# Attention passes: five edge columns of a round copied out of a turned node table in SBUF instead of four of them being gathered by GpSimd and one by ScalarE's DMAs

## Chip, cores, metric

One Trainium2 chip, one core. The metric is the device time of one launch in microseconds (us), as the median over runs. Engine names: PE is TensorE, DVE VectorE, ACT ScalarE, POOL GpSimd, SP SyncE.

## What is computed

Four graph networks follow one another on 12,500 nodes of 64 features and 200,000 edges sorted by destination. The change touches the three attention layers in the middle (stages c3, c4 and c5 and what lies between them). Cut to its core, such a layer is:

```python
h = x @ W                                   # per node, 4 heads of 16
e = (h * a_s)[src] + (h * a_d)[dst]         # per edge and head (c3 adds a term of edge_attr)
e = leaky_relu(e, 0.2)
w = exp(e - segment_max(e, dst))
out = segment_sum(w * h[src], dst) / segment_sum(w, dst)
```

Every edge needs the row of its source node: 64 projected features and 4 scores. Nodes are laid out as node = p * 98 + c (128 partitions p, NC = 98 columns c), edges as edge = p * 1563 + t, so that one *column* t is 128 edges, one on each partition, with 128 unrelated source nodes.

## The kernel before, in words

**Tables.** The node stages (conv_to_gat, gat_to_gat) end in gat_back (L1396): for a block of up to eight node columns, PE turns pairs of columns of h (L1415), ACT copies the turned pair to a small buffer hn (L1435), PE multiplies it by wg = [W, W a_s, W a_d] for both nodes of the pair (L1426), and ACT copies the result to gt (L1441). gt is stored to g_tab in DRAM, one row of TG = 72 floats for a node (64 features, 4 source scores, 4 target scores); POOL also scatters the target scores to ad_start (L1457).

**An attention pass** is gat_edges (L1805). It takes the 1563 edge columns in NGRP = 98 groups of GW = 16 columns, through a ring of NY = 6 slots of the buffer y (slot = group mod 6). Six groups are a *round*; there are 16 rounds and two groups more, which are handled as four half pieces (LASTS). For each group:

- POOL fills the slot by one indirect DMA for each column (L1862), after the piece that used the slot six groups before has been weighted (`weighted`). It takes all columns but those of the list `taken`: SP fetches column 15 of slots 2 and 5, ACT column 14 of slot 5. So POOL has 93 of 96 columns of a round.
- SP fetches a column by loading 32 source places at a time into registers (L303) and issuing 128 one-row DMAs (L307). ACT does the same for its column in four parts of 32, in the first four groups of a round, each after its other work of the group (`group`, L2009).
- DVE's `step` (L1880 to L1943) adds the scores (L1894; in c3 also the edge term that PE made, L1899), applies the leaky relu (L1903), makes running maxima by four scans (L1909), carries the last one (L1918, which waits until ACT has sent the piece before), forms the exponents' arguments (L1921 to L1925), waits for ACT's exponentials (L1930), weights the rows (L1931), sums them by a scan over 1156 elements (L1938) and carries on (L1941).
- ACT's `weights` makes the exponentials (L1979, L1984), `send` waits for the scan and copies maxima and sums to `row` (L1992, L1993), and issues the store (L1996). In c3 it also issues the load of edge_attr (L1999).

The order is written out by hand on each engine, and each runs a hardware loop over rounds: DVE and ACT both go through the six groups of a round in one loop body. DVE and ACT are tied within a group: exponentials wait for `shifted` (L1925), weighting waits for the exponentials, sending waits for the scan. Nothing else is planned by cost.

**Between c2 and c3** stands block_diagonal (L1787), in which POOL cuts a small matrix with two instructions (L1798, L1801) while no other engine has work.

Of the kernel before, what the change touches and what calls it, by code (L numbers as in the profile page):

```python
# [18 lines left out]
F32 = mybir.dt.float32  # L19
I32 = mybir.dt.int32  # L20
# [5 lines left out]
P = 128  # L26
# [31 lines left out]
ACT_SLOT, ACT_K, NACT = NY - 1, GW - 2, NGRP // NY  # L58
NTABLE = NSYNC + NACT
# [9 lines left out]
    ln_squared ln_var ln_rooted ln_inverted ln_done w_made ones_set h_turned0 h_turned1 mixed0 mixed1 q_ready0  # L69
    q_ready1 edges_ready q_turned0 q_turned1 weighted0 weighted1 row_ready0 row_ready1 q_filled q_carried multiplied  # L70
    scored maxed m_carried shifted exps r_ready summed carried differed fix_steps agg_made0 agg_made1 agg_turned0
    agg_turned1 agg_copied0 agg_copied1 done0 done1 den inv inv_has skipped0 skipped1 gat_steps cut ad_filled
# [3 lines left out]
    norm_steps w_zeroed new_turned hn_ready g_mixed gt_ready skipped own_scored same_copied  # L76
""".split()
# [44 lines left out]
def by_pool(g, taken):  # L122

    return width(g) - taken.count(g % NY)
# [27 lines left out]
def over_wide_blocks(eng, body):  # L152

    with eng.Fori(0, NWBLK // 2) as i:
        for b in range(2):
            body(i, b)
    for b in range(NWBLK % 2):
        body(NWBLK // 2, b)

# [15 lines left out]
class Stage:  # L175
# [38 lines left out]
    def row_slots(self, fills, taken=(), cut=0):  # L214

        return [[self.dma(f"gathered_{slot}{part}", fill_of(slot, taken) * n - cut * part * (slot == HALVED[1]))
                 for part in range(1 + (slot in HALVED))] for slot, n in enumerate(fills)]

    def pass_slots(self, taken, ahead=0):

        return self.row_slots([len(range(slot, NGRP, NY)) - (slot < ahead) for slot in range(NY)], taken, CUT)
# [14 lines left out]
def build(nc, a, out):  # L236
# [149 lines left out]
    def begin(y, wq_t, bq, wk_t, bk, we_t):  # L386
# [35 lines left out]
        src_loaded, places_stored = st.dma("src_loaded", 32), st.dma("places_stored", 32)  # L422
# [17 lines left out]
        with nc.Block(no_gpsimd_drain=True) as block:  # L440
            @block.sync
            def _(sp):
# [7 lines left out]
                with nc.allow_non_contiguous_dma("single columns of src"):  # L450
                    by_column = a["src"].rearrange("(p t) -> t p", p=P)
                    sp.dma_start(src_i[0:NSYNC, :], by_column[(EVERY - 1) * GW + SYNC_K:EVERY * GW * NSYNC:EVERY * GW, :])\
                        .then_inc(src_loaded.h, 16)
                    sp.dma_start(src_i[NSYNC:NTABLE, :], by_column[ACT_SLOT * GW + ACT_K:NY * GW * NACT:NY * GW, :])\
# [74 lines left out]
            def _(v):  # L529
# [144 lines left out]
                v.wait_ge(*src_loaded(32))  # L674
# [675 lines left out]
    def gat_weights(st, w, a_src, a_dst, heads, edge=None):  # L1350


        wg, wr = st.sb("wg", [P, 2, TG]), st.sb("wr", [P, D])
# [1413 lines left out]
```

## Time and profile before

| | us |
|---|---|
| median of 3 runs (lowest, highest) | 13215.1 (13211.56, 13216.55) |
| the profiled execution, from its first to its last instruction | 13211.9 |
| POOL busy | 9802.5 (74%) |
| DVE busy | 6811.8 (52%) |
| ACT busy | 4061.7 (31%) |
| PE busy | 517.1 (4%) |
| POOL's gathers of the three passes (L1862), busy and issue gaps | 4291.3 + 1386.9 |

The profiled execution's span is 3.2 us below the median of the runs, which is a launch's time with what lies around the span. The page's busy shares are means over stages: the passes of the change take about 5,700 us of the span. In them POOL is busy for three quarters of the time, and the rest of its time is the gap between one gather and the next. Busy time counts neither register instructions nor loads of registers nor the issue of a DMA; the queue of an engine is written with a q behind its name (ACTq, SPq).

### The profile page before, as it was taken

What the parts mean: (1) busy time and instruction counts of PE and PEld (TensorE: products, weight loads), DVE (VectorE), ACT (ScalarE), POOL (GpSimd) and SP (SyncE); (2) the same over time, 40 slices, a digit from 0 to 9 for tenths busy, and PEclk for the clock granted to TensorE, in tenths of its full rate; (3) what the DMA queues carried; (4) which work ended last, traced back from release to release, by engine and by line L of the source; (5) the groups of instructions that cost most, each with busy time, mean ns of one, the idle gap of its engine ahead of it and who ended that gap; (6) DMA issues with size and microseconds to landing.
All of it is one profiled execution on the core that took longest, in us unless ns stands there. A gap on an engine that the chain in (4) does not pass through costs nothing. (4 is left out here: it accounts for less than half of the span.)

```text
span 13211.9 us, 103483 instructions
## 1 busy us (share of the span) xinstructions
PE 517.1 (4%) x1768; PEld 338.5 (3%) x1768; DVE 6811.8 (52%) x10645; ACT 4061.7 (31%) x4014; POOL 9802.5 (74%) x10362
## 2 busy tenths in 40 slices
PE   3000001100000200000010000000000000000001
PEld 1000000100000200000000000000000000000000
DVE  2777876377777533333333333343333336656656
ACT  4333333233333311111111111111111113666663
POOL 7777776777777677777777777777777776777775
PEclk9999999555555655555555555555555555555555
DMA  8445444344444222222212222222222223444443
GB/s 334 120 123 129 123 123 107 90 123 123 123 122 124 64 66 65 63 65 66 63 45 61 61 63 62 60 49 58 62 61 61 61 63 89 160 160 156 162 160 116
DMA packets 977609, 1316.81 MB, mean 100 GB/s; under 512 B 660939, under 2 KB 676770, under 8 KB 963551
## 3 DMA queue, kind: packets, MB, share of 16 engines
q10 hardware_dynamic: 558595, 803.76, 18.8%
q0 software_dynamic: 334400, 373.85, 14.8%
q1 hardware_dynamic: 83996, 134.02, 2.8%
q14 instruction: 604, 4.95, 0.1%
q8 instruction: 14, 0.23, 0.0%
HBM read 651.23 MB, written 659.53 MB: 99 GB/s over the span
## 5 line engine op out<-in xcount | busy, mean ns | idle before, releaser
L1862 POOL DMA_INDIRECT c_y<-g_tab,srcs x4545 | 4291.3, 944 | 1386.9 <-issue 1386.9
L2318 POOL DMA_INDIRECT c_y<-h_tab,srcs x1547 | 1461.0, 944 | 506.4 <-issue 471.4
L824 POOL DMA_INDIRECT c_y<-h_tab,srcs x1531 | 1444.9, 944 | 467.1 <-issue 467.1
L824 POOL DMA_INDIRECT first_y<-h_tab,srcs x1452 | 1370.6, 944 | 445.2 <-issue 442.6
L1894 DVE TENSOR_TENSOR c_s<-c_y,c_ad 128x64 f32<-128x64 f32 x300 | 79.6, 265 | 1905.2 <-DMA c_y<-g_tab,srcs 1873.7
L1979 ACT ACTIVATE c_ex<-c_de 128x64 f32<-128x64 f32 x300 | 67.9, 226 | 3171.7 <-issue 2847.4
L1930 DVE COPY c_w_in<-c_ex 128x64 f32<-128x64 f32 x300 | 66.8, 223 | 1580.1 <-ACT c_ex L1979 1580.1
L1938 DVE TENSOR_TENSOR_SCAN c_acc<-c_r,c_w_in 128x1156 f32<-128x1156 f32 x300 | 753.9, 2513 | 10.4
L846 DVE TENSOR_TENSOR_SCAN c_q_all<-c_mask,c_q_in 128x408 f32<-128x408 f32 (+2 forms) x800 | 734.3, 986 | 16.3 <-issue 8.8
L890 DVE TENSOR_TENSOR_SCAN c_acc<-c_r,c_w_in 128x408 f32<-128x408 f32 (+2 forms) x800 | 732.0, 978 | 6.9
L939 ACT ACTIVATE c_q_in<-c_q_raw 128x1552 f32<-128x1552 f32 (+1 forms) x200 | 596.7, 2983 | 271.8 <-DVE c_q_in L906 197.5
L1993 ACT ACTIVATE c_row<-c_acc 128x1088 f32<-128x1088 f32 x300 | 618.2, 2061 | 0.0
L953 ACT ACTIVATE c_ex<-c_de 128x16 f32<-128x16 f32 (+1 forms) x200 | 37.4, 187 | 1781.8 <-DVE c_de L879 1781.8
L1931 DVE TENSOR_TENSOR c_w_in<-c_y,c_ex 128x1024 f32<-128x1024 f32 x300 | 581.9, 1940 | 0.0
L967 ACT ACTIVATE c_row<-c_acc 128x1552 f32<-128x1552 f32 (+1 forms) x200 | 564.8, 2824 | 0.0
L2362 DVE TENSOR_TENSOR_SCAN c_acc_s<-c_mask,c_su 128x442 f32<-128x442 f32 (+4 forms) x500 | 478.1, 1022 | 130.4 <-ACT c_su L2455 130.3
L2347 DVE TENSOR_TENSOR c_su<-c_y,c_ea_ps 128x1024 f32<-128x1024 f32 (+1 forms) x100 | 186.0, 1860 | 636.5 <-DMA c_y<-h_tab,srcs 636.5
L2368 DVE TENSOR_TENSOR_SCAN c_acc_m<-c_penm,c_mu 128x442 f32<-128x442 f32 (+4 forms) x500 | 475.4, 1015 | 0.0
L1992 ACT ACTIVATE c_row<-c_fm 128x64 f32<-128x64 f32 x300 | 92.1, 307 | 1124.8 <-DVE c_acc L1938 1124.8
L2464 ACT ACTIVATE c_row<-c_acc_s 128x2048 f32<-128x2048 f32 (+1 forms) x100 | 374.4, 3744 | 138.6 <-DVE c_acc_s L2362 138.6
L2466 ACT ACTIVATE c_row<-c_acc_m 128x2048 f32<-128x2048 f32 (+1 forms) x100 | 374.5, 3745 | 89.2 <-DVE c_acc_m L2368 89.2
L857 DVE TENSOR_TENSOR c_prod<-c_y,c_q_all 128x1552 f32<-128x1552 f32 (+1 forms) x100 | 173.3, 1733 | 365.3 <-DMA c_y<-h_tab,srcs 365.0
(405 smaller groups left out, 6432.2 us busy)
## 6 DMA issues: line engine op xcount, KB each, us to landing
c_y<-g_tab SPq DMA_DIRECT2D x12288, 0.3 KB
rows_d<-c_row ACTq DMA_DIRECT2D x96, 2048.0 KB, 6.9
rows_d<-c_row ACTq DMA_DIRECT2D x288, 576.0 KB, 2.9
c_q_raw<-q_start ACTq DMA_DIRECT2D x194, 776.0 KB, 6.2
rows_d<-c_row ACTq DMA_DIRECT2D x192, 784.0 KB, 4.3
c_y<-h_tab SPq DMA_DIRECT2D x6144, 0.2 KB
c_y<-g_tab ACTq DMA_DIRECT2D x6144, 0.3 KB
q_start<-first_y SPq DMA_DIRECT2D x97, 776.0 KB, 8.9
```

The lines of the kernel that those rows point to most:

```text
L824: nc.gpsimd.indirect_dma_start(y[:, g % NY, k, 0:D], None, h_tab, source(g, k))\
L846: last = v.tensor_tensor_scan(flat(qs[:, lo:hi]), flat(mk[:, 0:hi - lo]), flat(q_cur[:, lo:hi]), 0.0, ALU.mult, ALU.add)
L890: last = v.tensor_tensor_scan(flat(ac[:, lo:hi]), flat(rr[:, 0:hi - lo]), flat(w_cur[:, lo:hi]), 0.0, ALU.mult, ALU.add)
L939: act.activation(narrow(q_in[:, pc.b], pc.w)[:, :, 1:pc.w + 1], q_raw[:, pc.slot, pc.lo:pc.lo + pc.w].rearrange("p t f -> p f t"), ACT.Copy)
L967: act.activation(row[:, b, 0:w, 0:F], narrow(acc[:, b], w)[:, :, 1:w + 1].rearrange("p f t -> p t f"), ACT.Copy).then_inc(row_ready[b].h, 1)
L1862: nc.gpsimd.indirect_dma_start(y[:, g % NY, k, :], None, g_tab, source(g, k))\
L1931: v.tensor_tensor(w_heads[:, :, 0:JG, 1:w + 1], ys[:, :, 0:D].rearrange("p t (h j) -> p h j t", h=H), ex[:, :, 0:w].unsqueeze(2).to_broadc ...
L1938: v.tensor_tensor_scan(flat(ac), flat(rr), flat(w_cur), 0.0, ALU.mult, ALU.add).then_inc(summed.h, 1)
L1993: act.activation(row[:, b, 0:w, 0:F], narrow(acc[:, b], w)[:, :, 1:w + 1].rearrange("p f t -> p t f"), ACT.Copy).then_inc(row_ready[b].h, 1)
L2318: nc.gpsimd.indirect_dma_start(y[:, g % NY, k, :], None, h_tab, source(g, k))\
L2362: last = v.tensor_tensor_scan(flat(ac_s[:, lo:hi]), flat(mk[:, 0:hi - lo]), flat(su_c[:, lo:hi]), 0.0, ALU.mult, ALU.add)
L2368: last = v.tensor_tensor_scan(flat(ac_m[:, lo:hi]), flat(pm[:, 0:hi - lo]), flat(mu_c[:, lo:hi]), 0.0, ALU.add, ALU.max)
```

## The change

gat_back keeps the turned pairs: instead of a small buffer, ACT writes them in place over h, which after the stage holds, for node pair j and partition p, the 128 features of nodes (p, 2j) and (p, 2j + 1) as *column* j * 128 + p, that is on 128 partitions. wg is kept for the pass as well.

A column of 128 edges can then be made without DRAM. An engine copies, edge by edge, the turned column of the source's pair into a 128x128 buffer (128 copies of 128x1 with an address from a register), PE multiplies that buffer by wg, which gives the row of the even and of the odd node of the pair for each edge (128x144 in PSUM), and DVE takes one of the two by two multiplications with masks.

- ACT does this for three columns of a round (slots 3, 5 and 2), in two parts of 32 copies in every group: one between `weights` and `send`, one behind `send`. Its row fetches by DMA are gone.
- DVE does it for two columns of a round (slots 4 and 2), in 2, 1, 1, 2, 1, 1 parts of 32 copies in the six groups: the first of a group stands between L1925 and L1930, a second one at the end of the step.
- The two tasks for slot 2 prepare the *next* round (late), so in the first round POOL fetches those columns.
- POOL has 89 of 96 columns of a round left (91 in the first). SP's two columns stay.
- The choice by masks (`choose`, five in a round, two instructions and three waits each) and a copy of the round's masks stand at the ends of DVE's steps. The masks and the places of the pairs come from DRAM: ACT loads the places for both engines, four small DMAs in a round.
- PE's loop is written out over the six groups, with five more multiplications in a round.
- block_diagonal becomes gat_tables: POOL's two instructions as before, beside a chain of 19 DVE steps on small tiles, a turn on PE and two stores by SP, which make masks_d and picks_d.

ACT's `pick_part` is the same as DVE's with `activation(..., Copy)` for the copies. The diff, cut (`spread` is PE's, `pick_part` and `choose` DVE's, the last hunk ACT's):

```diff
-ACT_SLOT, ACT_K, NACT = NY - 1, GW - 2, NGRP // NY
+ACT_TASKS, ACT_PARTS = [Task(3, GW - 1, 0), Task(5, GW - 2, 0), Task(2, GW - 2, 1)], [2, 2, 2, 2, 2, 2]
+DVE_TASKS, DVE_PARTS = [Task(4, GW - 1, 0), Task(2, GW - 3, 1)], [2, 1, 1, 2, 1, 1]
...
 def gat_back(st, gt, wg, ps_h, h_ready):
-        hn = st.sb("hn", [P, 2, 4, P])
+        def turned(i):
+            c, n = BLOCKS[i]
+            return h[:, c:c + n, :].rearrange("p (j s) f -> p j (s f)", s=2)
...
-            act.activation(hn[:, i % 2, 0:m, :], ps_h[:, 0:m, :], ACT.Copy).then_inc(hn_ready.h, 1)
+            act.activation(turned(i), ps_h[:, 0:m, :], ACT.Copy).then_inc(hn_ready.h, 1)
...
-        taken = SYNC_SLOTS + [ACT_SLOT]
+        taken, late = SYNC_SLOTS + [t.slot for t in TASKS], [t.slot for t in TASKS if t.late]
...
+                def spread(pick, rows_, n, q):
+                    pe.wait_ge(*pick.picked(n * pick.m + q + 1))
+                    pe.nop(nofuse=True)
+                    pe.wait_ge(*pick.chosen(n * (2 * pick.m) + 2 * q))
+                    pe.nop(nofuse=True)
+                    nc.tensor.matmul(pick.ps, rows_[:, q * P:(q + 1) * P], wg[:].rearrange("p k f -> p (k f)"),
+                                     start=True, stop=True).then_inc(pick.spread.h, 1)
...
+                def pick_part(n, q, part):
+                    ...
+                    v.nop(nofuse=True)
+                    _, nodes = nc.values_load_multi_w_load_instructions(
+                        v_at[:, q * P + part * NREG:q * P + (part + 1) * NREG], [mybir.EngineType.DVE], ...)
+                    for k, node in enumerate(nodes, q * P + part * NREG):
+                        last = v.tensor_copy(v_rows[:, k:k + 1], turned[:, bass.ds(node, 1)])
+                    if part == NPART - 1:
+                        last.then_inc(by_dve.picked.h, 1)
+
+                def choose(pick, n, q):
+                    e, t, ps = pick.entry + q, pick.tasks[q], pick.ps
+                    to = y[:, t.slot, t.k, 0:TG]
+                    v.wait_ge(*pick.spread(n * pick.m + q + 1))
+                    v.tensor_scalar(to, ps[:, 0:TG], round_masks[:, e:e + 1], None, ALU.mult).then_inc(pick.chosen.h, 1)
+                    v.wait_ge(*pick.chosen(n * (2 * pick.m) + 2 * q + 1))
+                    v.scalar_tensor_tensor(out=to, in0=ps[:, TG:2 * TG], scalar=round_masks[:, NTASK + e:NTASK + e + 1],
+                                           in1=to, op0=ALU.mult, op1=ALU.add).then_inc(pick.chosen.h, 1)
+                    v.wait_ge(*pick.chosen(n * (2 * pick.m) + 2 * q + 2))
...
                     weights(piece(i, b))
                     if bd is not None:
                         act.wait_ge(*e_scored[b](i + 1))
                         edge_attrs(i + 1, b, ...)
+                    for q, part in parts[0:1]:
+                        pick_part(n, q, part)
                     send(piece(i, b))
-                    if j < NPART:
-                        if j == 0:
-                            act.wait_ge(*at_read(n * 16 + 16))
-                            act.nop(nofuse=True)
-                        part(j * NREG, ACT_SLOT, act_got)
+                    for q, part in parts[1:]:
+                        pick_part(n, q, part)
```

## Rows read from the trace of the kernel before

**Rows 1.** The page, groups: busy us, mean ns of one, idle time before and its releaser

```profile
L1862 POOL DMA_INDIRECT c_y<-g_tab,srcs x4545 | 4291.3, 944 | 1386.9 <-issue 1386.9
L1894 DVE TENSOR_TENSOR c_s<-c_y,c_ad 128x64 f32<-128x64 f32 x300 | 79.6, 265 | 1905.2 <-DMA c_y<-g_tab,srcs 1873.7
```

**Rows 2.** Line L1862 in pass c3: ns min/median/max, first and last start

```profile
L1862 POOL DMA_INDIRECT c_y<-g_tab,srcs x1515: 940/944/1008, 4685.9 to 6577.4; - x190
```

**Rows 3.** Timeline of c3's end on DVE: the last two half pieces

```profile
6576.04 0.21 DVE L1894 TENSOR_TENSOR c_s<-c_y,c_ad 128x32 f32<-128x32 f32 x1 [4.86 <-DMA c_y<-g_tab,srcs]
...
6584.19 0.22 DVE L1943 COPY carry_v<-c_acc 128x68 f32<-128x68 f32 x1
```

**Rows 4.** SP timeline in c3: columns that waited for nothing

```profile
5181.30 50.63 SPq L307 DMA_DIRECT2D c_y<-g_tab  x128
5234.79 0.23 SPq L323 DMA_DIRECT2D c_at<-places_d  x1
...
5290.20 49.74 SPq L307 DMA_DIRECT2D c_y<-g_tab  x128
```

**Rows 5.** Line L303, loads of 32 registers: ns min/median/max

```profile
L303 SPq TENSOR_LOAD <-c_at x700: 2023/2126/6043, 393.4 to 12906.1; - x175
L303 ACTq TENSOR_LOAD <-c_at x192: 3047/3137/3471, 4722.0 to 10846.7; - x192
```

**Rows 6.** Timeline of stage c1: small instructions with nothing between them

```profile
2221.52 0.15 DVE L874 COPY carry_m<-c_fm 128x1 f32<-128x1 f32 x1
2221.59 0.15 DVE L875 TENSOR_TENSOR c_de<-c_fm 128x3 f32<-128x3 f32 x1
...
2223.85 0.21 ACT L966 ACTIVATE c_row<-c_fm 128x3 f32<-128x3 f32 x1 [1.43 <-DVE c_acc L890]
...
2223.96 0.70 ACT L967 ACTIVATE c_row<-c_acc 128x291 f32<-128x291 f32 x1
```

**Rows 7.** Lines L1996, L2018, L1929, instructions of the queues: ns min/median/max

```profile
L1996 ACTq FUSED_REGOPS  x270: 46/52/60, 4721.3 to 10762.7; - x135
...
L2018 ACTq EVENT_SEMAPHORE  x48: 17/17/17, 4721.9 to 10781.0; - x48
...
L1929 DVEq EVENT_SEMAPHORE  x300: 21/21/21, 4712.2 to 10903.4; - x150
```

**Rows 8.** Timeline of a group of c3 on ACT

```profile
5430.54 0.23 ACT L1979 ACTIVATE c_ex<-c_de 128x64 f32<-128x64 f32 x1 [14.88 <-issue]
...
5435.56 0.31 ACT L1992 ACTIVATE c_row<-c_fm 128x64 f32<-128x64 f32 x1 [3.80 <-DVE c_acc L1938]
5435.77 2.11 ACT L1993 ACTIVATE c_row<-c_acc 128x1088 f32<-128x1088 f32 x1
5438.06 0.39 ACTq L1996 DMA_DIRECT2D rows_d<-c_row  x1
5441.69 11.21 ACTq L307 DMA_DIRECT2D c_y<-g_tab  x32
```

**Rows 9.** Lines L1979 and L1941: ns min/median/max

```profile
L1979 ACT ACT_TABLE_LOAD  x30: 1283/1283/1283, 4712.6 to 8497.0; - x30
...
L1941 DVE COPY c_w_in<-c_acc x297: 224/227/461, 4718.9 to 10901.9; 128x68 f32<-128x68 f32 x149
```

**Rows 10.** Timeline of the same group on DVE

```profile
5424.47 0.27 DVE L1894 TENSOR_TENSOR c_s<-c_y,c_ad 128x64 f32<-128x64 f32 x1 [10.99 <-DMA c_y<-g_tab,srcs]
...
5426.53 0.22 DVE L1925 TENSOR_TENSOR c_de<-c_de,pen 128x64 f32<-128x64 f32 x1
5430.80 0.23 DVE L1930 COPY c_w_in<-c_ex 128x64 f32<-128x64 f32 x1 [4.05 <-ACT c_ex L1979]
...
5432.96 2.56 DVE L1938 TENSOR_TENSOR_SCAN c_acc<-c_r,c_w_in 128x1156 f32<-128x1156 f32 x1
```

**Rows 11.** Timeline around c2's end and c3's first step: start, us, engine, line

```profile
4684.09 0.12 DVE L1945 MEMSET c_w_in<- 128x68 f32 x1 [18.12 <-PEq L1794]
...
4710.01 0.27 DVE L1894 TENSOR_TENSOR c_s<-c_y,c_ad 128x64 f32<-128x64 f32 x1 [0.45 <-DVE c_r L1959]
```

More of the change, by code:

```diff
@@ L119, in width, with by_pool @@
     return GL if g == NGRP - 1 else GW
-def by_pool(g, taken):
-    return width(g) - taken.count(g % NY)
+def by_pool(g, taken, late=()):
+    return width(g) - taken.count(g % NY) + (late.count(g) if g < NY else 0)
 def fill_of(slot, taken):
@@ L158, in over_wide_blocks, with is_round, __init__, parts_in @@
         body(NWBLK // 2, b)
+def is_round(n, at):
+    return isinstance(n, int) and n == at
+class Picker:
+    def __init__(self, st, who, tasks, counts, entry):
+        self.tasks, self.m, self.entry = tasks, len(tasks), entry
+        at = [0]
+        for n in counts:
+            at.append(at[-1] + n)
+        assert at[-1] == NPART * self.m and len(counts) == NY
+        self.parts = [[divmod(p, NPART) for p in range(at[j], at[j + 1])] for j in range(NY)]
+        self.ended = [[q for q, part in self.parts[j] if part == NPART - 1] for j in range(NY)]
+        assert all(tasks[q].late for q in self.ended[NY - 1])
+        self.cut = -(-self.m // 2)
+        self.batches = [range(0, self.cut), range(self.cut, self.m)]
+        total = sum(ROUNDS - t.late for t in tasks)
+        self.picked, self.spread = st.sem(f"picked_{who}", total), st.sem(f"spread_{who}", total)
+        self.chosen = st.sem(f"chosen_{who}", 2 * total)
+        self.at_got = [st.dma(f"places_{who}{b}", 16 * ROUNDS) for b in range(2)]
+    def parts_in(self, n, j):
+        return [(q, part) for q, part in self.parts[j] if not (is_round(n, ROUNDS - 1) and self.tasks[q].late)]
+    def ended_in(self, n, j):
+        return [q for q in self.ended[j] if not (is_round(n, ROUNDS - 1) and self.tasks[q].late)]
+    def used_up(self, j):
+        return [b for b, qs in enumerate(self.batches) if qs[-1] in self.ended[j]]
+    def chosen_in(self, n, j):
+        return [(q, n - (j == 0)) for q in self.ended[j - 1] if j or not is_round(n, 0)]
+def in_rounds(eng, body):
+    body(0)
+    with eng.Fori(1, ROUNDS - 1) as n:
+        body(n)
+    body(ROUNDS - 1)
 class Chain:
@@ L1860, in _ @@
                         pool.nop(nofuse=True)
-                    for k in range(by_pool(g, taken)):
+                    for k in range(by_pool(g, taken, late)):
                         nc.gpsimd.indirect_dma_start(y[:, g % NY, k, :], None, g_tab, source(g, k))\
```

271 lines of the change are left out of this document (206 added, 65 removed).

## The prediction, written before the changed kernel ran

> **What bounds the kernel now.** First the page's groups, for the engine that is never free. POOL's 4545 gathers of the three passes take 4291.3 us, and the 1386.9 us idle before them have one releaser, issue: POOL never waited for a buffer, and a gather costs it (4291.3 + 1386.9) / 4545 = 1.249 us. DVE stood 1873.7 us for those gathers to land [rows 1]. Then one pass by its first and last gather: 1515 of them start from 4685.9 to 6577.4, which is 1.249 us apiece again [rows 2]; c4 and c5 have the same count (4545 is 3 x 1515), and the mean over all three is the same. So each pass is POOL's 1515 columns and an end: c3 ends with DVE's last copy at 6584.4 [rows 3], 1898.5 us after its first gather. A round of six groups is 93 x 1.249 = 116.2 us. Then the engines beside it, for their slack, because the change fills it. All durations are from one execution with a span of 13211.9 us; the median of the runs is 13215.1, so I subtract from that one and carry the 3.2 us between them along.
>
> **POOL's term.** Four columns fewer in 16 rounds, less the two late ones of the first round: 62 a pass, 186 in all, x 1.249 = 232 us. POOL's round becomes 89 x 1.249 = 111.2 us. This is the whole gain, and it is had only if everything else fits in 111.2 us.
>
> **SP** is not changed, but its room shrinks. Two columns that waited for nothing, with a loop end between them, took from 5181.30 to 5290.20, 108.9 us [rows 4]. They fit, with 2.3 us left. The same rows price a loop's end: 2.9 us from the last DMA at 5231.93 to the next place load at 5234.79, against 0.3 within a body, so 2.5 us.
>
> **ACT's round.** One part is a load of 32 registers, 3.14 us [rows 5], and 32 copies of 128x1. ACT issued the next small instruction 0.11 us after one of 3 elements [rows 6]; before each copy stands a register operation that makes the address, 52 ns on this queue [rows 7], which runs while the engine works. So 0.11 us each, 6.7 us a part with 0.05 for the nop. Ends: 0.09 (shorter operand) and 0.16 (nothing hidden). The rest of a group is 0.25 to the load behind the exponentials and 2.9 from the send's start at 5435.56 to its DMA issue's end at 5438.45; the sum of L1984 and the waits is hidden by the part between [rows 8]. A group is 0.25 + 6.7 + 2.9 + 6.7 = 16.6; a round 6 x 16.6 + 2.5 loop end + 1.3 table load [rows 9] + 4 DMAs of 0.3 = 104.6 us; c3 has a DMA more in a group, 0.4 each, 107. It drops 128 row DMAs, a burst of 11.21 us and its load in four groups [rows 8]. Alone it fits.
>
> **DVE's round.** The engine issues 128x1 copies 0.07 us apart [rows 6], faster than its queue can make addresses. Address operation and copy: ACT's 52 ns, times 21/17 for the two queues' semaphore instruction [rows 7], plus 0.07 = 0.13 us; ends 0.07 (all hidden) and 0.18. A load of 32 registers isn't in the trace for DVE. Rows give 2.13 on SP and 3.14 on ACT [rows 5]; with the same 21/17 that is 2.6 to 3.9. I take 3.2, their middle, since no row says which of the two DVE resembles. A part is 3.2 + 0.05 + 32 x 0.13 = 7.4 us, eight a round. The rest of a group: 2.3 us to the exponents' arguments (2.0 without L1899, in c4 and c5), 4.7 from L1930 to the scan's end at 5435.52, 0.3 to the next step [rows 10]. Five choices of two dependent instructions on 72 elements are 0.7 each by rows of that size (0.22 to 0.27 and the handover), the masks 0.35. Sum 6 x 7.0 + 8 x 7.4 + 3.5 + 0.35 + 2.5 = 107.6, less 1.5 because a part's load begins some 0.25 before L1925 ends: 106 us. Alone it fits, too.
>
> **Together they don't quite.** Each engine's parts stand in the way of the other. In a group with one DVE part, DVE runs 7.15 + 4.7, and the next group's L1918 must wait for ACT's row copies, which end 2.4 behind the scan (2.11 and 0.21 [rows 8]), plus 0.65 to the arguments: 15.0 us. ACT's second part then makes it late, and the second such group goes at ACT's 16.6. A group with two DVE parts (the first and fourth) is 7.15 + 4.7 + 0.3 + 0.7 + 7.4 + 2.0 = 22.3. Half a round is 22.3 + 15.0 + 16.6 = 53.9, a round 107.8, plus 2.5 loop end, 0.7 for the first group's second choice, 2.1 for ACT's table load and place loads that come on this path: 113.1 us, and 114.5 in c3, where a group has an instruction on DVE and a DMA on ACT more. That is 2 to 3 us over POOL's 111.2. POOL, five groups ahead, loses its lead and begins to wait for `weighted`.
>
> **A pass then** runs from the first gather: 24.1 us to the first step (4710.0 - 4685.9 [rows 2, 11]), 2.5 for the masks, which ACT asks for only behind the target scores (my estimate, as no row has such a load alone; its ends of 1 and 4 us move the sum by 4.5), 16 rounds, and 18.3 for four half pieces, of which the last two took 8.4 [rows 3]. c3: 44.9 + 1832 = 1876.9, 21.6 less than 1898.5. c4 and c5: 44.9 + 1809.6 = 1854.5, 44.0 less each. Sum -109.6.
>
> **Small terms.** gat_tables: 19 dependent steps of some 0.3 us, a turn and two stores, about 9 us; DVE stands idle for 18.12 us there, until POOL has issued the last scatters [rows 11], so nothing; 9 us if that cover were gone. gat_back loses a wait and no instruction. PE's five multiplications a round stand behind the picks and a group ahead of their use; it is 4% busy. Fewer one-row DMAs: nothing, as nobody waited for ACT's column.
>
> **Forecast:** 13215.1 - 109.6 = 13105.
>
> **Rivals.**
> (A) *POOL stays the bound.* If DVE's load is 2.6, or ACT's copies are 0.09, a round of the pair is within a us of 111.2 and the groups' slack takes the rest. Time 13215 - 232 = 12983. For it: each engine alone has 4 to 7 us of room. The Trainium skill (ScalarE: Activation LUTs, What ACT_TABLE_LOAD costs) gives an activation 186 ns plus 0.833 an element and an overlap of 93, thus 94 ns here by estimate; by that the sum would be near 12995, while the row says 111 ns at three elements.
> (B) *The forecast*, rounds of 112 to 115: 13035 to 13185.
> (C) *Slower: the queue of DVE is the bound.* Its place is the load of registers and the address before each copy. At 3.9 us for the load a part is 8.1, half a round gains 1.4 in the two-part group, and the round is 116.1 (117.5 in c3): c3 +26, c4 and c5 +4 each, 13249. With copies of 0.15 as well, rounds are 118.7 and 120.2, 13376. It turns at a round of (1898.5 - 44.9) / 16 = 115.9, a DVE part of about 8.1 instead of 7.4, so a small miss decides. For it: DVE's semaphore instruction takes 21 ns where ACT's takes 17 [rows 7], and ACT's load is the dearer of two [rows 5]. The Trainium skill (Advanced Engine Details and Errata, Clock Domains) puts DVE's sequencer at 0.96 GHz and ACT's at 1.2, which by that page would turn ACT's load into 3.9, this case; the trace agrees in the semaphore rows, and shows no load on DVE.
> (D) *DVE's copies hold POOL up.* 256 copies a round of 0.15 us [rows 6]: if each held a gather for half of that, POOL's round would be 111.2 + 19 = 130 and the time near 13900; it turns at 18 ns a copy. The Trainium skill (SBUF — State Buffer, Who interferes with whom) says that copies with source and target in SBUF can take a port pair that DVE shares with GpSimd, whose descriptor writing then stands still. Against it: L1941 is such a copy, 297 times beside the gathers, and their median is 944 ns with a maximum of 1008 in c3 [rows 2, 9].
> That the change does not do what it says I give nothing: POOL's count falls by construction.
>
> **How the numbers follow.** A 0.27, B 0.34, between B and C within 0.2% 0.08, C 0.28, D 0.03. Within 0.2% (26 us) is about what a measurement of this kernel can tell from no change. Faster 0.61, same 0.08, slower 0.31. The range must hold both signs: from 12975, A with some us for shorter issue, to 13390, C with dear copies; D and copies of 0.18, or ACT's at 0.16, lie outside with about 0.12. The forecast's own range is B's.
>
> **What would show it.** L1862's count 4359 and its idle time: only issue means A; waits for L1931 of 1 to 3 us a round mean B, of 5 and more C. Loads of registers on DVE: 3.2, or 2.6, or 3.9. Distance of 128x1 copies: 0.13 on DVE, 0.11 on ACT. First and last gather of c3: 1813 us apart in A, some 1855 in B. Gathers longer than 944 at the median mean D. I am wrong if a round is neither POOL's nor the pair's, as when SP's columns, now 2.3 us short of the round, take longer, or if instructions of bodies three times as long come too slowly.

## The result, and the profile after

| | us |
|---|---|
| median before, 4 runs (lowest, highest) | 13213.3 (13210.3, 13216.6) |
| median after, 4 runs (lowest, highest) | 12978.7 (12973.1, 12979.4) |
| ratio after to before, 95% interval | 0.982 (0.981 to 0.983) |
| forecast, range | 13105, 12975 to 13390 |
| the profiled execution of after: span | 12971.1 |

The change gains 234.6 us. The forecast was 110, and rival A's time, 12983, is within 5 us of what came. The page's groups of the changed kernel (busy us, mean ns of one, idle time before and its releaser):

```profile
L2005 POOL DMA_INDIRECT c_y<-g_tab,srcs x4359 | 4115.3, 944 | 1329.7 <-issue 1329.7
L2221 ACT ACTIVATE c_ad_raw<-h 128x1 f32 x18048 | 1847.7, 192 | 1484.1 <-issue 1484.1
L2056 DVE COPY c_ad_raw<-h 128x1 f32 x11904 | 1384.8, 154 | 883.7 <-issue 883.7
L2086 DVE TENSOR_TENSOR c_ad_raw<-c_y,c_ad 128x64 f32<-128x64 f32 x300 | 79.7, 266 | 855.6 <-DMA c_y<-g_tab,srcs 816.7
```

POOL has the 4359 gathers that were counted, at (4115.3 + 1329.7) / 4359 = 1.249 us, the price of [rows 1], and still waits for issue alone: it never waited for a buffer. DVE's wait for gathers fell from 1873.7 us to 816.7 and did not vanish: 17 us of every round (816.7 / 48) are still free on DVE. The two lines of copies give the price of a part, its loads with it: (1384.8 + 883.7) / 372 = 6.10 us on DVE and (1847.7 + 1484.1) / 564 = 5.91 on ACT. Pass c3 by its first and last gather, and its last instruction on DVE:

```profile
L2005 POOL DMA_INDIRECT c_y<-g_tab,srcs x1453: 940/944/1007, 4679.8 to 6493.6; - x182
```

```profile
6500.39 0.22 DVE L2137 COPY carry_v<-c_acc 128x68 f32<-128x68 f32 x1
```

Against [rows 2, 3] the pass is 1820.8 us instead of 1898.5, 77.7 less. c4 and c5 have 1820.7 and 1820.2 by the same two rows, 77.8 and 78.0 less. That is 233.5 of the 234.6 us. The two profiled executions are 240.8 us apart; 6.1 of the rest lie ahead of c3's first gather, where executions of one and the same kernel differ, too (it starts at 4679.8 here and at 4683.7 in e4, which ran the same instructions). Waits of DVE in 1200 us of c3 (us in total, times, longest):

```profile
DVE c_ad_raw L2056 <- issue: 207.6, 121, 3.0
DVE c_ad_raw L2086 <- DMA c_y<-g_tab,srcs: 160.8, 43, 7.2
```

There is no wait of L2110 for ACT's row copies (L2196) among them, the wait on which the forecast's coupling stood. SP's columns in c3, which I had put at 108.9 us for two [rows 4]:

```profile
5172.06 49.64 SPq L361 DMA_DIRECT2D c_y<-g_tab  x128
...
5279.92 49.36 SPq L361 DMA_DIRECT2D c_y<-g_tab  x128
```

Two of them take 5279.92 - 5172.06 = 107.9 us here.

### The profile page after: what moved, and what is told of

Its sections match the earlier page's. It is cut to its first block and busy times, and to the rows that moved or that the text cites. A ratio compares the mean times of both kernels' runs of the same rounds, so it can differ in the third digit from the quotient of the medians.

```text
span 12971.1 us, 155321 instructions
## 1 busy us (share of the span) xinstructions
PE 700.2 (5%) x2237; PEld 457.9 (4%) x2237; DVE 8317.3 (64%) x23091; ACT 5864.4 (45%) x22034; POOL 9626.1 (74%) x10176
## 5 line engine op out<-in xcount | busy, mean ns | idle before, releaser
L2005 POOL DMA_INDIRECT c_y<-g_tab,srcs x4359 | 4115.3, 944 | 1329.7 <-issue 1329.7
L2221 ACT ACTIVATE c_ad_raw<-h 128x1 f32 x18048 | 1847.7, 192 | 1484.1 <-issue 1484.1
L2056 DVE COPY c_ad_raw<-h 128x1 f32 x11904 | 1384.8, 154 | 883.7 <-issue 883.7
L2086 DVE TENSOR_TENSOR c_ad_raw<-c_y,c_ad 128x64 f32<-128x64 f32 x300 | 79.7, 266 | 855.6 <-DMA c_y<-g_tab,srcs 816.7
L2196 ACT ACTIVATE c_row<-c_acc 128x1088 f32<-128x1088 f32 x300 | 618.3, 2061 | 0.0
```

The source lines that it names most:

```text
L2005: nc.gpsimd.indirect_dma_start(y[:, g % NY, k, :], None, g_tab, source(g, k))\
L2056: last = v.tensor_copy(v_rows[:, k:k + 1], turned[:, bass.ds(node, 1)])
L2196: act.activation(row[:, b, 0:w, 0:F], narrow(acc[:, b], w)[:, :, 1:w + 1].rearrange("p f t -> p t f"), ACT.Copy).then_inc(row_ready[b].h, 1)
L2221: last = act.activation(a_rows[:, k:k + 1], turned[:, bass.ds(node, 1)], ACT.Copy)
```

## The experiments

Each is an edit of the changed kernel; times are medians of 4 to 10 runs (e9 and e10: one run), and differences are against runs of the kernel before on the same chip (13211.5 to 13214 us, 13232 for e9 to e12). A part's price is always (busy + idle) / count of the copies' line, as above. The length of a round is read from DVE's copy of the round's masks, one in each of the 16 rounds of a pass: (last start - first start) / 15. In c4 of the change and of e13:

```profile
L2083 DVE COPY c_ad_raw<-c_ad_raw x16: 172/173/365, 6808.2 to 8475.1; 128x10 f32 x14, 128x10 f32<-128x10 f32 x2
```

```profile
L2090 DVE COPY c_ad_raw<-c_ad_raw x16: 173/173/410, 6857.5 to 8552.1; 128x10 f32 x14, 128x10 f32<-128x10 f32 x2
```

That is 111.1 and 113.0 us. The table sets two sums beside the measured rounds. (What the pair DVE and ACT needs beyond the longer of its two queues is called coupling here.) *Longest queue* is the longest of three: POOL's 111.2, DVE's 48.35 + 8 parts (50.15 in c3), which is the prediction's sum for DVE alone without its 1.5 us of overlap, and ACT's 24.2 + 12 parts (26.6 in c3). *Coupled* is the prediction's sum for the pair, 2 x (22.3 + 15.0 + the longer of DVE's 15.0 and ACT's group) + 5.3 (1.4 more in c3), with the run's parts in place of its own, and never under 111.2. A measured part of DVE is net of the 0.25 us by which a load begins ahead of the end of L1925, so it stands against 7.2 us, the prediction's 7.4 less 1.5 / 8.

| run | DVE part | ACT part | against before, us | rounds of c3, c4, c5 | longest queue c3, c4 | coupled c3, c4 |
|---|---|---|---|---|---|---|
| the change | 6.10 | 5.91 | -234.6 | 111.2, 111.1, 111.1 | 111.2, 111.2 | 111.2, 111.2 |
| e14, ACT dearer | 6.11 | 6.94 | -235.5 | 111.2, 111.1, 111.1 | 111.2, 111.2 | 111.2, 111.2 |
| e13, DVE dearer | 7.75 | 5.91 | -181.8 | 115.3, 113.0, 112.4 | 112.1, 111.2 | 115.6, 114.2 |
| e5, both dearer | 8.05 | 6.94 | -36.4 | 118.1, 115.7, 115.9 | 114.5, 112.8 | 120.4, 119.0 |
| e11, DVE dearer | 8.27 | 5.91 | -27.5 | 119.1, 116.3, 116.1 | 116.3, 114.5 | 119.8, 118.4 |
| e10, ACT dearer still | 6.47 | 7.74 | -25.6 | 119.4, 115.5, 115.9 | 119.5, 117.1 | 114.1, 112.7 |
| e12, DVE, store moved | 9.16 | 4.30 | +241.3 | 124.4, 123.2, 122.3 | 123.4, 121.6 | 126.9, 125.5 |
| e6, DVE dearer | 9.40 | 5.92 | +361.8 | 126.0, 125.2, 124.5 | 125.3, 123.5 | 128.8, 127.4 |
| e3, both, ACT most | 8.13 | 8.55 | +441.9 | 128.9, 125.6, 125.5 | 129.2, 126.8 | 127.3, 125.9 |

**One engine's share alone.** e1 keeps ScalarE's tasks, e2 VectorE's.

```diff
-DVE_TASKS, DVE_PARTS = [Task(4, GW - 1, 0), Task(2, GW - 3, 1)], [2, 1, 1, 2, 1, 1]
+DVE_TASKS, DVE_PARTS = [], [0] * 6            # e1; e2: ACT_TASKS, ACT_PARTS instead (and column 14 for 13)
```

> Only ScalarE's three columns are made from the turned table; VectorE copies none, and GpSimd fetches those two itself (91 of 96 columns of a round). Theory 1 (POOL is the only bound, and a column costs it 1.249 us): 31 columns fewer a pass than before, 93 in all, 13213.3 - 116 = 13097, a pass 38.7 us shorter. Theory 2 (the two engines' parts hold each other up): nothing of it is left here, as DVE has no part; the same 13097. Theory 3 (part of the gain of the whole change comes from elsewhere than from POOL's columns, say from fewer DMAs of ScalarE): under 13085, since ScalarE's 128 row DMAs a round are gone here too.

> Only VectorE's two columns are made from the turned table; ScalarE makes none and fetches none (92 of 96 columns left to POOL, against 93 before). Theory 1 (POOL's columns alone): 15 fewer a pass, 45 in all, 13213.3 - 56 = 13157. Theory 2 (DVE's parts delay the steps): alone they fit by every price, the same 13157; slower than 13170 would mean that DVE's copies do hold the steps or POOL's gathers up. POOL's gathers stay at 944 ns if DVE's copies do not disturb them.

Measured 13092.8 and 13153.9 us, 121.1 and 60.0 less than before. POOL's line of each page:

```profile
L2005 POOL DMA_INDIRECT c_y<-g_tab,srcs x4452 | 4202.8, 944 | 1358.1 <-issue 1358.1
```

```profile
L2005 POOL DMA_INDIRECT c_y<-g_tab,srcs x4500 | 4258.7, 946 | 1373.7 <-issue 1373.7
```

Both gains are POOL's columns at 1.249 us (93 and 45 of them) within 5 us. Together they are 181 us for 138 columns, 1.31 us each, where the change has 234.6 for 186, 1.26 each (the 48 between them stand for the column that ACT fetched before). Theory 3 of the first run falls.

**The prediction's prices put in.** Registers are loaded again and used in place of the first ones.

```diff
+nodes = again(nodes, v_at, q * P + part * NREG, 24, mybir.EngineType.DVE)          # DVE, each part
+nodes = again(nodes, a_at, q * P + part * NREG, more, mybir.EngineType.Activation) # ACT: 22 and 8
```

> The changed kernel with its parts made as dear as the prediction had them: after the load of 32 registers DVE loads 24 of them again (2.10 + 1.5 or so, a part of 7.4 instead of 5.85 us), ScalarE loads 22 again in the first part of a group (6.7 instead of 5.25) and 8 again in the second (6.7 instead of 6.2). Theory 1 (the forecast's coupling was right and only its prices were off): the pair's round comes out over POOL's 111.2 again; by the prediction's sum 13105, by a closer replay of the waits step by step 13073; POOL's gathers wait for L-weighted in most rounds. Theory 2 (the slack between the engines takes it even at those prices, so the coupling itself was wrong): 12979 to 12990, and POOL never waits.

Measured 13655.8, 442 us slower than before, which no theory had. The second load's line shows why:

```profile
L1992 ACTq TENSOR_LOAD <-c_ad_raw x564: 542/2620/4739, 4712.0 to 11309.8; - x188
L1992 DVEq TENSOR_LOAD <-c_ad_raw x372: 1595/1597/2378, 4711.5 to 11270.6; - x186
```

DVE's 24 registers took 1.60 us, ACT's 22 took 4.7 in the first parts. ACT's part was 8.55 us, and by the prediction's own sum for ACT (104.6 at 6.7, so 24.2 + 12 parts) its queue alone needs 126.8 us a round, in c3 129.2 (measured 125.6 and 128.9). It had become the bound.

> The changed kernel with DVE's load of 32 registers made twice in every part: a part of 7.95 instead of 5.85 us, ScalarE's as they were. Theory 1 (coupling as in the forecast, with measured prices for ScalarE): by the forecast's sum a half round of 23.35 + 15.4 + 15.4 = 54.2, rounds of 113.7 and 115.2, thus 13133; by the replay of the waits 13031. Theory 2 (DVE's wait of some 17 us a round for gathers takes all of it): 2.1 x 8 = 16.8 us a round more, just within that wait, 12979. Theory 3 (it is added to every round in full, because the steps do not wait where the parts stand): 13213.3 - 234 + 3 x 16 x 16.8 = 13785.

The compiler dropped the first load, as all its registers were loaded again; what ran was the changed kernel once more, at 12976.2 us. Nothing follows for the theories.

```diff
-    pick_part(n, q, part, 22)
+    pick_part(n, q, part, 24)
```

> The run before with these prices had one that was not meant: in the first part of a group ScalarE's second load, of 22 registers, took 4.7 us and not 1.5, so that part came to 9.9 us instead of 6.7. Here that load is of 24 registers, as on DVE, where it took 1.60. Parts then: DVE 7.5, ScalarE 6.85 and 6.75, the prediction's 7.4 and 6.7 within 0.15. Theory 1 (the coupling was right, the prices off): by the replay of the waits step by step, rounds of 115.0 in c3 and 113.6 in c4 and c5, 13214 - 104 = 13110; by the prediction's own sum 13105. Theory 2 (the slack takes it): 12979. Theory 3 (the 22-register load was not the reason, and parts of these prices already cost what that run showed): 13600 and more.

Measured 13175.7, ratio 0.997 (0.996 to 0.998). Theory 2 falls; theory 1 has the sign and is 66 us short. The part on DVE was not 7.5 but (1384.5 + 1610.1) / 372 = 8.05 us, so the run does not test the forecast at its own prices. Theory 3 falls with the 22-register load. What DVE waited for in ten rounds of c4:

```profile
DVE c_ad_raw L2063 <- issue: 342.6, 110, 5.1
DVE c_ad_raw L2093 <- issue: 31.3, 10, 3.3
...
DVE c_w_in L2131 <- ACT c_ex L2189: 12.0, 10, 1.5
DVE c_fm L2117 <- ACT c_row L2203: 11.6, 20, 0.7
```

For ACT it waited 2.4 us a round. This is the coupling as the trace has it. The 3.1 us ahead of L2093 are the loop's end, which the prediction had at 2.5.

> DVE's parts alone made dear: behind its load of 32 registers it loads 24 and then 16 again, 5.85 + 1.60 + 1.07 = 8.5 us a part, ScalarE's as in the changed kernel (5.25 and 6.2). This is dearer than the 8.1 at which rival C put the turn to slower. Theory 1 (coupling, replayed step by step with the measured prices): rounds of 117.0 and 115.6, so 13214 + 1 = 13215, no gain left. Theory 2 (the prediction's sum with these prices: 24.45 + 16.0 + 16.0 a half round, rounds of 118.2 and 119.7): 13350. Theory 3 (DVE's wait for gathers absorbs it): DVE waits some 17 us a round, 8 x 2.65 = 21.2 is wanted, 4 us a round over, 13213 - 234 + 3 x 16 x 4 = 13171.

Measured 13573.9, ratio 1.028. All three theories are far off, the replay of the waits by 359 us. Page lines, and DVE's wait for ACT's row copies in 1200 us of c3:

```profile
L2011 POOL DMA_INDIRECT c_y<-g_tab,srcs x4359 | 4114.1, 944 | 1757.0 <-issue 1313.0
L2064 DVE COPY c_ad_raw<-h 128x1 f32 x11904 | 1384.5, 154 | 2111.2 <-issue 2111.2
```

```profile
DVE c_fm L2118 <- ACT c_row L2204: 3.0, 10, 0.3
```

A part cost 9.40 us. And DVE stood for ACT 3.0 us in these 1200: at this price of DVE's part there is no coupling to speak of. With the prediction's terms for DVE alone (six groups of 7.0, or 7.3 in c3; choices 3.5, masks 0.35, loop end 2.5; eight parts) the round is 48.35 + 8 x 9.40 = 123.5, in c3 125.3; measured 125.2 and 126.0. So the new theory is the plainest: **a round is about the longest of the queues, each by itself**. The table bears it out within limits. It misses the round by at most 3.6 us below and 1.6 above. The coupled sum is 0.3 to 3.3 us too long where DVE is the bound and up to 5.3 us too short where ACT is (c3 of e10). What the longest queue leaves out where DVE is the bound, 1 to 4 us, is in part a real coupling, and the coupled sum has too much of it.

**Room below 111.2.** POOL is spared three more columns, which nobody fetches (that part of the output is left out).

```diff
+left = [(3, GW - 2), (4, GW - 2), (5, GW - 3)]
+taken = SYNC_SLOTS + [t.slot for t in TASKS] + [s_ for s_, _ in left]
```

> Three columns more of every round are fetched by nobody (column 14 of slots 3 and 4, column 13 of slot 5 stay zero), so POOL has 86 columns a round, 107.4 us; that part of the output is left out. It asks what binds next, and how much room the pair has. Theory 1 (SP is next, at the 108.9 us of its two columns; the pair's own round is 101.8, in c3 103.1): 13213.9 - 363 = 12851, and POOL waits for L-weighted about 1.5 us a round. Theory 2 (only POOL's columns count): 13213.9 - 330 x 1.249 = 12802. Theory 3 (the pair has no such room and binds just under 111): 12960 or more.

Measured 12798.7, 413 less: theory 2, 330 x 1.249 = 412. SP in c3:

```profile
5170.47 50.05 SPq L361 DMA_DIRECT2D c_y<-g_tab  x128
...
5278.04 49.50 SPq L361 DMA_DIRECT2D c_y<-g_tab  x128
```

Its two columns take 107.6 us, level with POOL's 86 x 1.249 = 107.4; the 108.9 of [rows 4] were no floor. Over the three passes DVE waits 262.5 us for SP's columns and 227.6 for POOL's, so SP is next. The pair fits in 107.4 as well.

**Where the slow loads come from, and what ACT's store has to do with them.** In the changed kernel, one stretch of c3: the issue of the row store, and the loads on three queues that begin right behind it (the last one behind the next store, whose issue ended at 5423.9):

```profile
L2199 ACTq DMA_DIRECT2D rows_d<-c_row x1: 362/362/362, 5408.2 to 5408.2; - x1
...
L2217 ACTq TENSOR_LOAD <-c_ad_raw x1: 2945/2945/2945, 5408.6 to 5408.6; - x1
...
L2052 DVEq TENSOR_LOAD <-c_ad_raw x1: 3023/3023/3023, 5409.2 to 5409.2; - x1
...
L357 SPq TENSOR_LOAD <-c_at x1: 3233/3233/3233, 5423.8 to 5423.8; - x1
```

Other loads take 1.97, 2.10 and 2.12 us on ACT, DVE and SP. In e9 the store is issued behind the second part:

```diff
 send: ...
-    act.wait_ge(*row_ready[b](pc.i + 1)); act.dma_start(by_edge(rows)...)
+def store(pc): ...            # the two, called at the group's end, behind parts[1:]
```

> The changed kernel, with ScalarE issuing the store of its rows behind the second part of a group instead of ahead of it. In the changed kernel a register load that begins within 0.6 us of the end of that store's issue takes 2.9 us on ScalarE (192 loads) and some 3.1 on DVE, where others take 1.97 and 2.10. Theory 1 (a load is slower while the store of 576 KB runs, whatever its engine): ScalarE's second-part loads fall to 1.97, and whichever loads now begin right behind the store, the first part's included, rise to 2.9. Theory 2 (a load is slower because a DMA issue stands right ahead of it in its own queue): only loads behind an issue on the same queue are at 2.9, and none on DVE or SP. Time: POOL's columns are as before, 12979 by both.

12997.6 us in one run against 13232.4 on that chip, 234.8 less, as the change itself. The load between the row copies and the store, and SP's load right behind the store's issue (5420.64 to 5421.00):

```profile
L2220 ACTq TENSOR_LOAD <-c_ad_raw x1: 1972/1972/1972, 5415.4 to 5415.4; - x1
...
L357 SPq TENSOR_LOAD <-c_at x1: 3092/3092/3092, 5421.0 to 5421.0; - x1
```

Over the whole of e9, loads that begin within 0.6 us behind the end of a store's issue have medians of 2.96 to 3.16 us on ACT (72 of them), DVE (14) and SP (13), and ACT's 420 that begin more than 2.5 us behind it 1.97. So it is theory 1: the load's place against the store decides, on whatever queue. The edit has a second effect, since ACT's load now runs while the engine still makes the row copies: its part fell from 5.91 to (1828.5 + 574.0) / 564 = 4.26 us.

> DVE's parts alone at the prediction's price: behind the load of 32 registers a load of 24 again, 5.85 + 1.60 = 7.45 us against the 7.4 predicted; ScalarE's parts as in the changed kernel. Theory 1 (once DVE's parts are coupled to ScalarE's sending, its first load of a group starts right behind ScalarE's row store and takes 3.1 us instead of 2.1, which keeps the pair coupled): replay 13213 - 60 = 13153, rounds of 114.8. Theory 2 (loads stay at 2.1 and the coupling alone counts): rounds of the pair just under 111.2, thus 12979. The prediction's own sum with DVE at 7.45 and ScalarE at its measured prices: half round 22.35 + 15.0 + 15.0, rounds of 110.0 and 111.5: 12985.

Measured 13204.9, ratio 0.998 (0.997 to 0.999).

```profile
L2011 POOL DMA_INDIRECT c_y<-g_tab,srcs x4359 | 4124.9, 946 | 1375.6 <-issue 1317.4
L2063 DVE COPY c_ad_raw<-h 128x1 f32 x11904 | 1384.5, 154 | 1691.5 <-issue 1691.5
```

Theory 2 and the 12985 of the prediction's sum fall; theory 1, 60 us less than before, is 32 us short. A part came to 8.27 us, 0.8 more than counted: nearly half of the parts are some 0.35 us longer by a pause within the copies, and loads beside the store take a us more. By the queue alone 48.35 + 66.2 = 114.5, in c3 116.3; measured 116.3 and 116.1, and 119.1 in c3.

> DVE's parts of 8.5 us as in the run that took 13574, but with ScalarE's row store issued behind its second part, away from the start of DVE's loads. Theory 1 (DVE's loads in that run were 1 us slower because they began beside the row store): most of that goes, and ScalarE gets its second load in beside its row copies; replay 13213 + 60 to + 75, so about 13280, 13200 to 13350. Theory 2 (the place of the store does not matter for DVE): within 60 us of 13574.

Measured 13473.7, 120 us less than e6 against before (+241.3, +361.8), and not the 290 less of the replay. Both theories fall: the first has 13200 to 13350, the second no more than 60 us of difference. DVE's part fell to 9.16 us:

```profile
L2064 DVE COPY c_ad_raw<-h 128x1 f32 x11904 | 1384.5, 154 | 2022.3 <-issue 2022.3
```

372 parts x 0.24 us = 89 of the 120 us: the place of the store matters that much for DVE's parts. Where the other 31 lie was not traced. Queue alone 121.6, measured 123.2 and 122.3.

**Which price decided.** e13 has 16 registers again on DVE, e14 the second loads on ACT alone.

> DVE's second load is of 16 registers instead of 24 (1.09 us instead of 1.60). Parts of the run before had 0.35 us more than I had counted, in every second of them a pause within the copies, and loads beside the row store at 3.1; so a part is here 7.1 to 8.3 us, and this is the run in which it stands nearest to the prediction's 7.4; ScalarE's as in the changed kernel. Theory 1 (the pair's own round crosses POOL's 111.2 between parts of 6.1 and 8.2 us): rounds of 112 to 113 in two of the passes or all, replay 13212 - 154 to - 226, about 13020, range 12985 to 13110. Theory 2 (the forecast's sum at its own price of DVE's part): 13105. Theory 3 (POOL's lead takes it all): 12979.

> ScalarE's parts alone at the prediction's price: a second load of 24 registers in the first part and of 8 in the second, 7.0 and 7.0 us a part; DVE's parts as in the changed kernel. Theory 1 (DVE's part is the term that decides): POOL stays the bound, 12979 to 12990. Theory 2 (the forecast's weight on ScalarE's second part, which made the second one-part group go at ScalarE's 16.6): a half round of 19.2 + 15.0 + 17, rounds of 107 and 109 with the ends, still under 111.2. Rival (ScalarE's price does couple the pair): 13050 or more.

Measured 13029.8, ratio 0.986 (0.985 to 0.988), and 12976.0. The page lines of e13, and then of e14:

```profile
L2011 POOL DMA_INDIRECT c_y<-g_tab,srcs x4359 | 4118.7, 945 | 1329.2 <-issue 1327.1
L2063 DVE COPY c_ad_raw<-h 128x1 f32 x11904 | 1384.4, 154 | 1497.0 <-issue 1497.0
```

```profile
L2228 ACT ACTIVATE c_ad_raw<-h 128x1 f32 x18048 | 1846.0, 192 | 2067.2 <-issue 2005.5
```

ACT's part at 6.94 us, above the predicted 6.7, changes nothing while DVE's is 6.11. This does not speak against the forecast's coupling, whose sum gives 107.3 for it, also under 111.2: e14's theories 1 and 2 both hold, and only its rival falls. DVE's part at 7.75, above the predicted 7.4, costs 53 us of the 234.6, 42 of them in c3. Of e13's theories the first holds (range 12985 to 13110), and the second, the forecast's 13105, is 75 us too long.

e13 is the run to study, because its rounds are the forecast's: 115.3, 113.0 and 112.4 us, where the forecast had 114.5, 113.1 and 113.1, the same mean of 113.6. And yet the gain is 181.8 us instead of 110, and c4, at rounds 1.9 us longer than in the change, is only 7.0 us longer (1827.8 against 1820.8). The rest is made good in the last round. From its mask copy to the end of the pass it is 85.2 us here and 108.3 in the change. In c4 of e13, from that copy on, the last scans of full groups and the last copy:

```profile
8552.10 0.17 DVE L2090 COPY c_ad_raw<-c_ad_raw 128x10 f32<-128x10 f32 x1
...
8593.06 2.56 DVE L2139 TENSOR_TENSOR_SCAN c_acc<-c_r,c_w_in 128x1156 f32<-128x1156 f32 x1
...
8607.50 2.56 DVE L2139 TENSOR_TENSOR_SCAN c_acc<-c_r,c_w_in 128x1156 f32<-128x1156 f32 x1
...
8615.61 2.56 DVE L2139 TENSOR_TENSOR_SCAN c_acc<-c_r,c_w_in 128x1156 f32<-128x1156 f32 x1
...
8637.12 0.22 DVE L2144 COPY carry_v<-c_acc 128x68 f32<-128x68 f32 x1
```

The last three full groups follow 14.4 and 8.1 us behind one another, where earlier rounds have 23 and 16. They have no parts: the tasks for slot 2 prepare the next round, and the last round has none. That takes four of the eight parts from DVE and four of the twelve from ACT.

The time that DVE loses does not show as waits of POOL either (2.1 us in all). The ring of six slots lets the gathers run five groups, over 90 us, ahead of the steps, and in e13 the steps never fall that far behind: POOL finishes its gathers, and the steps end late. c3's last gather starts at 6499.2 and its last copy at

```profile
6547.15 0.22 DVE L2144 COPY carry_v<-c_acc 128x68 f32<-128x68 f32 x1
```

48 us behind it, where the changed kernel has 6.8.

**Forms of a load.**

```diff
+again(nodes, a_at, lo, *[(10, 32), (8, 30), (10, 30), (12, 32), (9, 32), (8, 32)][j], ...)
```

> Why a load of 22 registers took 4.7 us. ScalarE makes a second load in the first part of each of the six groups, of 22, 22, 20, 20, 23 and 24 registers, starting 10, 8, 10, 12, 9 and 8 places (of 4 bytes) behind a multiple of 32, and one of 8 registers, 24 places on, in the second parts. Theory 1 (the start decides: multiples of 4 places are cheap): 1.5 us for starts of 8 and 12, over 4 for 9 and 10. Theory 2 (the count decides: multiples of 4 or 8 are cheap): 1.3 to 1.6 for 20 and 24, over 4 for 22 and 23. Time: no more than the run with the 4.7 us load in all groups, 13656.

One round of c3: 22 registers from place 10, 22 from 8, 20 from 12, 24 from 8 (ns):

```profile
L1991 ACTq TENSOR_LOAD <-c_ad_raw x1: 4740/4740/4740, 5319.4 to 5319.4; - x1
...
L1991 ACTq TENSOR_LOAD <-c_ad_raw x1: 1713/1713/1713, 5340.3 to 5340.3; - x1
...
L1991 ACTq TENSOR_LOAD <-c_ad_raw x1: 1259/1259/1259, 5378.7 to 5378.7; - x1
...
L1991 ACTq TENSOR_LOAD <-c_ad_raw x1: 1495/1495/1495, 5417.4 to 5417.4; - x1
```

20 from 10 took 4.31 us and 23 from 9 4.94. Theory 1: the start decides. From a place that is a multiple of four a register costs some 0.063 us (1.259 / 20), from another 0.215. The count has a share, too: 22 from place 8 took 0.45 us more than 20 from 12, as if the two beyond a multiple of four went at the dearer price.

The one run took 13206.8 us, 25.6 less than before. ACT's parts were (1845.9 + 2518.5) / 564 = 7.74 us and DVE's 6.47, and DVE waited 95.1 + 38.6 us for ACT in ten rounds of c4: here ACT's queue is the bound, 117.1 us by its sum and 119.5 in c3, measured 115.5 and 119.4.

**A sixth column.** ScalarE gets a fourth task, with the store behind the parts as in e9.

```diff
-ACT_TASKS, ACT_PARTS = [Task(3, GW - 1, 0), Task(5, GW - 2, 0), Task(2, GW - 2, 1)], [2, 2, 2, 2, 2, 2]
+ACT_TASKS = [Task(3, GW - 1, 0), Task(5, GW - 2, 0), Task(4, GW - 2, 1), Task(2, GW - 2, 1)]
+ACT_PARTS = [3, 4, 2, 2, 3, 2]               # DVE_PARTS = [1, 2, 1, 1, 2, 1]
```

> A sixth column is moved off POOL: ScalarE gets a fourth task (column 14 of slot 4, prepared for the next round), with 3, 4, 2, 2, 3, 2 parts in the six groups, DVE 1, 2, 1, 1, 2, 1, and ScalarE issues the store of its rows behind the last part of a group instead of ahead of the second, so that its register loads no longer stand behind a DMA issue (1.97 instead of 2.9 us). Theory 1 (replay of the waits): c4 and c5 follow POOL's 88 columns, 109.9 us a round; c3 the pair, 111.5: 13213.9 - 267 = 12947. Theory 2 (POOL's columns alone, 15 fewer a pass than in the changed kernel): 12979 - 56 = 12922. Theory 3 (ScalarE, with 16 parts of 5.25 beside 6 x 3.15, becomes the bound, loads stay at 2.9): rounds of some 115 and more, 13100.

Measured 12920.7, ratio 0.978 (0.977 to 0.979), 291.3 less than before. It beats both kernels:

```profile
L2008 POOL DMA_INDIRECT c_y<-g_tab,srcs x4314 | 4072.8, 944 | 1316.0 <-issue 1316.0
L2227 ACT ACTIVATE c_ad_raw<-h 128x1 f32 x23808 | 2428.8, 191 | 1027.0 <-issue 1025.5
```

POOL's columns alone (theory 2, 12922); its rounds are 110.2 us in all three passes, against 88 x 1.249 = 109.9. The replay's 111.5 for c3 was too long. ACT's part was (2428.8 + 1027.0) / 744 = 4.65 us, where the expectation has 5.25.

## Why the prediction was wrong

**POOL's term was right.** 186 columns x 1.249 = 232 us were forecast; the passes are 233.5 us shorter, and e1, e2, e7 and e8 gain what 93, 45, 330 and 231 columns cost at that price, within 5 us.

**SP's room** was read as 2.3 us from one pair of columns. It was 3.6 (e7), and in the changed kernel it did not bind.

**DVE's part was priced 7.4 us and measured 6.10.** The load was put at 3.2, the middle between SP's row and ACT's scaled by 21/17. The rows say 2.10 and 46 ns, and for ACT:

```profile
L2052 DVEq TENSOR_LOAD <-c_ad_raw x372: 2097/2104/3143, 4707.2 to 10574.6; - x186
...
L2217 ACTq TENSOR_LOAD <-c_ad_raw x564: 1951/2452/3248, 4707.8 to 10602.6; - x188
...
L2056 DVEq FUSED_REGOPS  x11904: 46/46/53, 4709.6 to 10580.6; - x199
...
L2221 ACTq FUSED_REGOPS  x18048: 37/37/43, 4710.1 to 10608.6; - x199
```

The 3.14 us of [rows 5] for ACT was not the engine's price: away from a row store ACT loads 32 registers in 1.97 us, and right behind its issue in 2.9. The copies came 0.115 us apart instead of 0.13 (3.71 us of 32), and nearly half of the parts have a pause of some 0.3 us that I had not counted. ACT's were 0.098 apart against 0.11. An address operation that is twice as wide as the semaphore instruction does not scale as it: the 52 ns of [rows 7] became 37 on ACT and 46 on DVE.

The Trainium skill (Advanced Engine Details and Errata, Clock Domains), from which the load would have come to 3.9 us on DVE, holds for the address operations (46 to 37 ns is 1.24, near the 1.25 of its 1.2 and 0.96 GHz) and not for the loads, 2.10 to 1.97. The estimate of 94 ns for a copy, from the Trainium skill (ScalarE: Activation LUTs, What ACT_TABLE_LOAD costs), is nearer to the measured 98 than my 111.

**Three steps failed.** The forecast missed the gain by 125 us. Either the first or the third, put right, gives rival A; the second, put right alone, gives a gain of some 180 us.

*"A part is 3.2 + 0.05 + 32 x 0.13 = 7.4 us."* It was 6.10, against 7.2 if both are net of the early load. With the measured parts my own coupled sum is 20.1 + 13.9 + 15.0 for a half round, 103 us a round, under POOL's 111.2: that is rival A.

*"16 rounds" in "A pass then".* The last round is not a whole one, as e13 shows. By my terms a pass is 15 rounds and 158.0 us in c4 (44.9 + 113.1); e13 has 15 rounds and 133.2. Over three passes that is 74 us, and e13's gain, at the forecast's rounds, is 72 us above the forecast. A pass bound by POOL hardly notices, since its gathers go on at their pace through the last round, and my 44.9 held there within a us or two.

*"Together they don't quite."* The prediction's prices keep each engine alone under 111.2, at 106 and 104.6 us; 7 us of coupling made 113.1 of it: the waits for ACT's row copies, 16.6 for the second one-part group, "which goes at ACT's", and 2.1 us of ACT's table and place loads. No run has just these prices, but those around them show less. DVE's rounds less their eight parts should leave 48.35 us without coupling (50.15 in c3) and 55.4 with mine. They leave 51.0 and 50.4 in c4 and c5 of e13 and 51.3 and 51.5 in e5, where ACT's part is above the predicted 6.7; in c3 53.3 and 53.7. That is 2 to 3.6 us and not 7. In c4, 1.7 of it in e13 and 2.4 in e5 are waits for ACT, and 0.6 are a longer loop end. By estimate, with the prediction's prices (8 x 7.2 = 57.7) the pair's round would have been 108 to 109 us in c4 and c5 and some 111.2 in c3: no longer than POOL's. What I overlooked stands in the trace of after on ACT, a wait of 4.26 us for DVE's scan ahead of its sending:

```profile
5395.28 0.23 ACT L2182 ACTIVATE c_ex<-c_de 128x64 f32<-128x64 f32 x1 [1.40 <-DVE c_de L2117]
...
5405.67 0.31 ACT L2195 ACTIVATE c_row<-c_fm 128x64 f32<-128x64 f32 x1 [4.26 <-DVE c_acc L2132]
```

ACT has a reserve in such groups, from which it can make its lateness good, and DVE asks for the exponentials only behind its own part. I added the slowest path of each group and never gave the reserve back. That this is where the difference went was not tested by a run of its own.

**Rival A** was right in its outcome. It had asked for a load of 2.6 on DVE; it was 2.10. **Rival C** was right in its mechanism, that DVE's queue decides when the part is dear. I put the turn to slower at a part of 8.1 us (7.9 as parts are measured); by e11 (8.27 us, -27.5) and 372 parts it stands at 8.3. That the two are so near is in part luck. Rival C counted a dearer part only in the two-part group; with the one-part group too, its sum reaches 115.9 us at 7.9 (7.7) already. And the short last round moves the turn up: e11 is still faster than before at rounds of 116.1 to 119.1, above the 115.9. That DVE's part was near no such price made the rival void.

**Rival D**: gathers have 944 ns at the median with 11904 copies beside them, and the issue gap is 0.305 us before and after; the port rule of SBUF — State Buffer (the Trainium skill, Who interferes with whom) shows no effect for copies of this size.

**What was to show it.** Count 4359 and only issue meant A, and so it was. The waits of POOL that I had named as the sign of B would have misled: e13 lost 53 us with 2.1 us of them. So would the first and last gather of c3: 1813.8 us apart in the change and 1814.8 in e13, whose rounds are the pair's.

## What to carry to other kernels

Sum up each engine's queue for a whole round first, and take the longest as the floor (here 0.7 to 3.6 us under the measured round where DVE was the bound); a chain through two engines adds to it only what is left when the waits that each has inside the round are used up. Then write out the first and the last round by themselves, for work that is prepared a round ahead is missing in one of them. A price taken from another engine's row must come from an instruction in the same surroundings: look at what stood just before it, and at what DMA ran beside it. When a producer has a lead of several buffers, look for lost time at the end of the pass, not in its waits.

## What the runs showed of the hardware that I had not expected

- A load of 32 registers from SBUF takes 2.10 us on DVE, 1.97 on ACT and 2.12 on SP. If it begins within half a us behind the end of the issue of the 576 KB row store, it takes about 3.0 on any of the three, and the delay is gone some 2 us behind it. Whether the store's reads of SBUF or its descriptors are what slows it was not tried.
- A load that starts on a place which is not a multiple of four costs 0.215 us a register, 3.4 times the 0.063 from an aligned place (e10). The kernel's own loads all start on such multiples.
- Copies with an address from a register pause once in nearly half of the parts (170 of 372 on DVE, 269 of 564 on ACT in the change); the engine is idle for 0.31 us on DVE and 0.17 on ACT, and the part is 0.35 and 0.27 us longer. What the queue waits for there stays open.
